# A graph network kernel: the last block's low halves laid beside its high halves

## The reference

```
edge_index = [src, dst]
# layer 0
msg  = (x[src] + rel_emb[type]) @ W_msg.T + b_msg
agg  = segment_sum(msg, dst) / max(deg, 1)
x    = layernorm(x + x @ W_self.T + b_self + agg)
# layers 1 and 2
h    = swish(segment_mean(x[src], dst) @ W1_l.T + b1 + x @ W1_r.T)
y    =       segment_mean(h[src], dst) @ W2_l.T + b2 + h @ W2_r.T
out  = layernorm(x + y)
```

## Time and profile before

| | |
|---|---|
| median of 3 runs | 366.36 us (366.32 to 366.43) |
| the profiled execution | 366.51 us, its span 364.7 us |
| PE busy | 335.0 us (92%), 3385 products |
| DVE busy | 232.8 us (64%) |
| ACT busy | 173.9 us (48%) |
| granted TensorE clock | 1.0 in nearly the whole span |

### The profile page before, as it was taken

How to read it: one execution, slowest core, us unless ns; L and a number is a source line. 1 busy time by engine, 2 the same in 40 slices (tenths; PEclk the granted TensorE clock), 3 DMA queues, 4 the chain that set the end, 5 groups by cost and what they waited for, 6 DMA issues and landing times.

```text
span 364.7 us, 9187 instructions
## 1 busy us (share of the span) xinstructions
PE 335.0 (92%) x3385; PEld 250.4 (69%) x3385; DVE 232.8 (64%) x597; ACT 173.9 (48%) x385; POOL 4.9 (1%) x17
## 2 busy tenths in 40 slices
PE   0689999999999999999999999999999999999970
PEld 0579998998998998998984454555474455455460
DVE  6999988998999999999446942330345031431454
ACT  1585667769778878778522141331252131121040
POOL 5000000000000000000000000000000000000000
PEclk9999999999999999999999999999999999999997
DMA  4700000000000000000000000000000001100102
GB/s 138 171 2 4 2 2 3 4 2 4 2 2 2 3 4 3 3 2 2 24 16 3 0 0 2 0 2 0 0 2 3 0 1 31 29 2 29 30 2 67
DMA packets 8523, 5.38 MB, mean 15 GB/s; under 512 B 370, under 2 KB 8476, under 8 KB 8476
## 3 DMA queue, kind: packets, MB, share of 16 engines
q1 hardware_dynamic: 8188, 4.32, 4.4%
q10 hardware_dynamic: 288, 0.43, 0.3%
HBM read 3.14 MB, written 1.60 MB: 13 GB/s over the span
## 4 chain that ended last, share of the span: by engine, by line
PE 84%; DVE 8%; ACT 4%; issue 2%; DMA 1%; ACTq 0%; DVEq 0%
PE ps L943 54%; PE ps L891 16%; PE ps L1009 5%; PE ps L1019 3%; PE ps L962 2%; ACT counts L834 2%; DVE hot L1182 1%; PE ps L989 1%; DMA counts<-dst_t 1%; PE ps L898 1%; PE ps L908 1%; DVE hot L1175 1%; DVE table L1192 1%; ACT new_first L812 1%; ACT scaled L790 1%
## 5 line engine op out<-in xcount | busy, mean ns | idle before, releaser
L943 PE MATMUL ps<-counts,table 128*128 128x256 f16 (+2 forms) x1350 | 214.6, 309 | 0.0
L943 PEld LDWEIGHTS ps<-counts,table 128*128 128x128 f16 x1350 | 114.9, 97 | 74.2 <-issue 0.2
L834 ACT CAST counts<-ps 128x494 f32 x208 | 107.7, 578 | 45.5 <-PE ps L891 44.9
L891 PE MATMUL ps<-hot 128*128 128x156 f16 (+1 forms) x584 | 67.9, 241 | 15.6 <-DVE hot L1182 15.0
L891 PEld LDWEIGHTS ps<-hot 128*128 128x128 f16 x584 | 53.1, 103 | 17.3 <-DVE hot L1182 15.3
L1182 DVE TENSOR_TENSOR hot<-iota,edges 128x1200 f16<-128x1200 f16 x73 | 56.6, 775 | 0.0
L1175 DVE TENSOR_TENSOR hot<-iota,edge_rows 128x768 f16<-128x768 f16 x73 | 40.1, 550 | 4.9 <-PE ps L928 4.6
L898 PE MATMUL ps<-window_hot,hot 128*128 128x19 f16 x292 | 42.5, 181 | 0.0
L1272 DVE TENSOR_TENSOR new_first<-ps,scaled 128x512 f32<-128x512 f32 (+1 forms) x9 | 5.4, 600 | 54.0 <-ACT scaled L790 54.0
L1272 DVE TENSOR_TENSOR hot<-ps,scaled 128x512 f32<-128x512 f32 (+1 forms) x8 | 5.1, 639 | 41.6 <-ACT scaled L790 41.6
L898 PEld LDWEIGHTS ps<-window_hot,hot 128*128 128x128 f16 x292 | 28.9, 99 | 0.7
(11 more groups left out here) (135 smaller groups left out, 320.3 us busy)
## 6 DMA issues: line engine op xcount, KB each, us to landing
table<-x SPq DMA_DIRECT2D x2, 768.0 KB, 5.1
out<-new_first SPq DMA_DIRECT2D x3, 256.0 KB
out<-hot SPq DMA_DIRECT2D x3, 256.0 KB, 2.4
counts<-first_dst ACTq DMA_DIRECT2D x1, 208.0 KB, 3.9
counts<-dst_t SPq DMA_DIRECT2D x1, 208.0 KB, 4.5
counts<-type_t ACTq DMA_DIRECT2D x1, 208.0 KB, 4.7
counts<-src_t SPq DMA_DIRECT2D x1, 208.0 KB, 5.0
hot<-w_l SPq DMA_DIRECT2D x2, 64.0 KB, 2.0
```

What stands on the lines that cost most here:

```text
L834: nc.scalar.copy(A[:, HALVES[half], bass.ds(bases[group % 8], GROUP_W)], window(group, half)).then_inc(copied[half], 1)
L891: return nc.tensor.matmul(window(group, half)[:, :, at[t]], row(tiles[t], LOW_AT, P), blocks_of(tiles[t], half), start=group == half == t ...
L943: last = nc.tensor.matmul(ps[:, sums_bank(q), first:first + width], table[:, b, part, :], A[:, b, at:at + width], start=b == part == 0, st ...
```

## The change

The last block's low half for the 53 nodes goes to rows 64 to 116 of the table's high part, so that one product over 128 rows covers both halves; for that the counts of rows 0 to 52 of the last block are copied to rows 64 to 116 by a DMA, once layer 0 no longer needs the relation counts that stood there. PE waits for the copy (semaphore `stacked`) ahead of the last block of chunk 7. In the later layers the last block then has one product in `aggregate`, and the turn of a 53-node chunk has one product, with an identity in which both halves stand (`ident_stacked`), made by one DVE instruction.

```
--- before.py
+++ after.py
@@ -246,7 +246,9 @@
         checks = later[:, 4 * D + 2 * CHUNK:4 * D + 2 * CHUNK + TILES]
         steps = later[:, 4 * D + 2 * CHUNK + TILES:4 * D + 2 * CHUNK + TILES + GROUPS]
         bias_last = later[:, 4 * D + 2 * CHUNK + TILES + GROUPS:][:, 0:D]
-        assert 5 * D + 2 * CHUNK + TILES + GROUPS <= (SLOTS - 1) * HOT_C * GROUP // 2
+
+        ident_stacked = later[:, 5 * D + 2 * CHUNK + TILES + GROUPS:].bitcast(F16)[:, 0:LAST]
+        assert 5 * D + 2 * CHUNK + TILES + GROUPS + P // 4 <= (SLOTS - 1) * HOT_C * GROUP // 2
 
         ident = new_first[:, 0:P]
         bias_msg = scaled_flat[:, 0:D]
@@ -281,9 +283,10 @@
             return (table1, table0)[layer_of(q)]
 
         def table_rows(table, q, part):
+
             first = chunk_of(q) * SUB
             if tiles_of(q) == 1:
-                return table[0:LAST, first, part, :]
+                return table[part * REL_ROW:part * REL_ROW + LAST, first, 0, :]
             return table[:, first:first + SUB, part, :]
 
         ps = ctx.enter_context(nc.psum_tensor("ps", [P, 8, 512], F32))
@@ -325,6 +328,7 @@
         x_in = [sem(f"x_in{k}") for k in range(2)]
         weights_in = sem("weights_in")
         late_weights_in = sem("late_weights_in")
+        stacked = sem("stacked")
         constants = sem("constants")
         pads_zero = sem("pads_zero")
         cleared = sem("cleared")
@@ -709,6 +713,13 @@
             sp.dma_start(bias_last, b2.rearrange("o d -> (o d)").partition_broadcast(P)
                          ).then_inc(late_weights_in, 16)
 
+
+
+            sp.wait_ge(agg_done, CHUNKS)
+            sp.wait_ge(deg_done, CHUNKS)
+            sp.dma_start(A[REL_ROW:REL_ROW + LAST, BLOCKS - 1, 0:N], A[0:LAST, BLOCKS - 1, 0:N]
+                         ).then_inc(stacked, 16)
+
             for q in range(2 * CHUNKS, ALL_CHUNKS):
                 sp.wait_ge(rows_ready, q + 1)
                 first = chunk_of(q) * CHUNK
@@ -939,11 +950,15 @@
                         pe.wait_ge(lo_ready, (layer_of(q) - 1) * CHUNKS + b // SUB + 1)
                     if b == first == 0 and summed_before(q) >= 0:
                         pe.wait_ge(sum_ready, summed_before(q) + 1)
-                    for part in range(2):
+                    both = q >= CHUNKS and b + 1 == BLOCKS
+                    if both and q == CHUNKS:
+                        pe.wait_ge(stacked, 16)
+                    for part in range(1 if both else 2):
                         last = nc.tensor.matmul(
                             ps[:, sums_bank(q), first:first + width], table[:, b, part, :],
                             A[:, b, at:at + width], start=b == part == 0,
-                            stop=b + 1 == BLOCKS and part == 1, skip_group_check=True)
+                            stop=b + 1 == BLOCKS and (both or part == 1),
+                            skip_group_check=True)
                     if b + 1 == BLOCKS and first + width == nodes:
                         last.then_inc(agg_done, 1)
 
@@ -956,13 +971,17 @@
                     pe.wait_ge(x_lo, (chunk_of(q) * SUB + SUB - 1) // X_PIECE + 1)
                 elif turn_bank(q) == messages_bank(q - 1):
                     pe.wait_ge(messages_scaled, q)
+                both = q >= CHUNKS and tiles_of(q) == 1
+                if both:
+                    pe.wait_ge(weights_ready, 4)
                 for t in range(tiles_of(q)):
                     size = min(P, nodes_of(q))
-                    for part in range(2):
+                    for part in range(1 if both else 2):
                         last = nc.tensor.matmul(
                             ps[:, turn_bank(q), t * P:t * P + size],
-                            table_in(q)[:, chunk_of(q) * SUB + t, part, :], ident_h[:, 0:size],
-                            start=part == 0, stop=part == 1, skip_group_check=True)
+                            table_in(q)[:, chunk_of(q) * SUB + t, part, :],
+                            ident_stacked if both else ident_h[:, 0:size],
+                            start=part == 0, stop=both or part == 1, skip_group_check=True)
                 last.then_inc(turned, 1)
 
             def count_degrees(q):
@@ -1452,6 +1471,9 @@
                     preset(POSTED)
 
             wait_copied(dve, GROUPS)
+            nc.vector.tensor_tensor(ident_stacked, ident_h[:, 0:LAST],
+                                    ident_h[:, REL_ROW:REL_ROW + LAST], ALU.add
+                                    ).then_inc(weights_ready, 1)
             nc.vector.memset(table1[32:REL_ROW, BLOCKS - 1], 0.0)
             nc.vector.memset(table1[REL_ROW:P, BLOCKS - 1], 0.0)
             for q in range(EARLY - 1, ALL_CHUNKS):
```

## The result

| | median | runs | ratio to before, 95% interval |
|---|---|---|---|
| before | 366.18 us | 16 | |
| changed | 369.50 us | 16 | 1.0094 [1.0073, 1.0115] |

The change makes the kernel 3.3 us slower; 368.5 us was forecast, from 366.4 to 371.5. The profiled executions differ by 3.2 us (369.67 against 366.51; spans 367.9 and 364.7). Line 957 is now the aggregation, 1028 and 1038 the dense products, 980 the turn. So beside the medians stands a second measure, which the groups don't touch: the time in the profiled execution from the first product of chunk 7 to the last restart of PE with eight products (191.33 to 352.68 us before, 161.35 us).

A forecast was written before the change was run, and what follows sets the result against it. PE's own work, mainly the aggregation, was taken to bound the later layers. Products removed -2.59, wait +3.4 and clock +1.35 sum to +2.2 us: 368.5 us against the 366.36 us median, range 366.4 to 371.5 us.

The forecast's parts named there:

- products removed: Chunks 7 to 12 and 14 to 19: one product of 0.216 us fewer each, all on the path, -2.59 us.
- the wait for the copy: PE at chunk 7's last block: wants the copy at 202.37 us, restarts at 205.8 us, +3.4 us.
- the clock: In or just behind PE's wait: falls to half for 2.7 us of products at double pitch, +1.35 us.
- the last steps: End of the kernel, behind PE's last restart: no term in the prediction, counted at 0.
- The two short chunks: Chunks 13 and 20, 53 nodes each: their savings only lengthen PE's idle time, counted at nothing; 0.1 us without that cover.
- VectorE's sum: Ahead of clearing the table at 179.98 us: 128 x 53 values, hidden by 0.81 us idle; at most 0.3 us otherwise.
- The copy on one engine: SP's copy of 53 rows: prime 53 leaves one DMA engine, share 0.06 to 0.07, like the kernel's last store.
- The straight line: Copy's streaming time, fitted through 512- and 1664-byte rows: 247 ns per 6250-byte row, 13.1 us for 53.
- The tail: After the copy's last packet: 0.3 us to landing, then 0.14 us until PE starts again.
- from issue to first packet: Start of SP's copy: 0.8 us, taken from the last 53-row store, first packet at 192.25 us.
- The two rates that I held as the long end: Slower paces for the copy: 22 GB/s gives a wait of 5.4 us, 14.6 GB/s one of 13.0 us.
- Rival (a): At chunk 7's last block: the copy waits but the clock holds, +0.8 us, 367.2 us; chance 0.33.

The follow-up runs named there:

- 64 rows: The changed kernel, with the copy taking 64 rows (the last 11 empty counts) instead of 53: 363.71 us, 0.9940 of the kernel before.
- the busy wait: The changed kernel, with 24 products of 384 columns into unused columns ahead of PE's wait for the copy: 367.71 us, 1.0050 of the kernel before.
- the copy alone: The kernel before, with only the 53-row copy and PE's wait for it added, two products per block everywhere: 372.01 us, 1.0164 of the kernel before.
- 59 rows: The changed kernel, copying 59 rows instead of 53: 370.66 us, 1.0128 of the kernel before.
- 58 rows: The changed kernel, copying 58 rows instead of 53: 363.19 us, 0.9923 of the kernel before.
- 54 rows: The changed kernel, copying 54 rows instead of 53: 364.13 us in one run, too few for a ratio.
- chunk 7's columns first: The changed kernel, its copy cut in two: chunk 7's 512 columns, then the rest with its own wait at chunk 8: 363.71 us, 0.9945 of before.

## Why the prediction was right

**Sign, mechanism and order of size were as forecast.** +2.2 us was predicted, +3.3 measured; each term against its measure:

| term | forecast | measured |
|---|---|---|
| products removed | -2.59 | -2.59 up to the last restart, -0.22 a chunk; -2.3 in the medians of 64 rows |
| the wait for the copy | +3.4 | +4.0 |
| the clock | +1.35 | +1.7 (the busy wait: 1.8 by medians, 1.66 by starts) |
| the last steps | 0 | +0.15 |
| sum | +2.2 | +3.3 |

**The saving.** 10.80 to 10.58 us a chunk is what one product fewer should give. Twelve make 2.59 us, and up to PE's last restart that is what the 64-row kernel gained, to 0.01 us; the medians show 2.3 us, with 1.2 to 3.2 as its interval. The two short chunks give nothing, their idle time is as long or longer: as forecast. Behind the last restart the span (taken to 0.01 us) goes on for 12.06 us before and 12.05 in the copy alone, but for 12.18 to 12.25 in the kernels with the stacked rows. The prediction had nothing for these 0.12 to 0.19 us, 0.15 in the table; what makes them was not tried. VectorE's sum took 0.19 us and its idle time shrank from 0.81 to 0.58: covered, as forecast.

**The copy on one engine.** The argument from the 53-row store held, and the numbers of rows around 53 show that it is the divisor and not the size: 53 rows 0.07, 59 rows 0.07 (over 192.80:207.20), 58 rows 0.14, 54 rows 0.54, 64 rows 0.86.

**The wait's size: the step that was mis-sized is the start.** The straight line gave 13.1 us of streaming; the packets run from 192.7 to 205.9 us, 13.2 us. The tail (0.3 + 0.14 us) was 0.45 us. But "from issue to first packet ... I take 0.8" was 1.3 us (191.40 to 192.7): the issue itself takes 0.69 us on SP, where the 53-row store took 0.26. That is 0.5 of the 0.6 us by which the wait was longer; that the longer issue makes the later start is not shown. The two rates that I held as the long end (22 and 14.6 GB/s) were too low: 331,250 bytes in 13.2 us is 25.1 GB/s (the 27 GB/s of the row 192.70:205.88 hold code packets too), where the straight line has 25.3.

By the Trainium skill's ceiling for the fabric (DMA: Bandwidth & Descriptors, "Where 436 GB/s comes from") the estimate was 27.2 GB/s for an engine and 12.2 us for the stream. The trace has 25.1 GB/s, under the ceiling, and a stream 1.0 us longer.

**The clock.** It fell, as the likelier case said, and cost 1.7 us and not 1.35: it was at half for 3.4 us of full work, not the 2.7 that I estimated. It fell at 206.5 us, that is just behind the wait and not in it, so that all of its time at half was paid for. The way to the estimate did not hold: I took the time at half to be as long as the idleness before the fall, but it was 3.4 us in the changed kernel, in the copy alone and with 59 rows, where PE had idled 3.9, 3.9 and 4.7 us before the fall. That 1.35 came near 1.7 is in part luck. Rival (a) (the clock holds) is what the kernel with the busy wait makes, 367.7 us, where 367.2 was given. The granted clock of the kernel before needs care at its start: it reads 1.00 from 20 to 28 us, while the products of the earlier trace rows took 312 ns in that stretch, the length that they have at 0.50 in the other profiles (315 ns from 22 to 24 us in the kernel with chunk 7's columns first); the product lengths that I read were the better guide.

**What stays open.** Why one DMA engine's copy starts 1.3 us behind its issue. What adds the 0.15 us at the end. Whether the forecast wait of 3.4 us would have made the clock fall. Whether single runs of the changed kernel left the wait without a fall: only one execution has a profile, but none of the 16 runs took less than 367.79 us, 3.3 us over the lowest of the kernel before (364.51), so nothing speaks for it.

## What to carry to other kernels

A partition count is part of the speed of a DMA from SP's queue: before a DMA whose landing is on the path, look at how many engines a transfer with that row count kept busy in the profile, and pad the rows to a number that more engines divide (64 here, and 54 or 58 were enough), or put the first-needed columns first. A saving that adds a wait is to be set against landing minus arrival, and to a wait of TensorE such as this one of 4.0 us the fall of the clock (here 1.7 us) is to be added. The change's worth lay in one row number: 53 gives +3.3 us, 64 gives -2.3. And where single runs fall in groups, a stretch of the profile between two fixed points shows what medians blur.

## What the hardware showed that I had not expected

- The same 53-row copy kept one DMA engine busy from SP's queue (0.07) and most of them from GpSimd's (0.68).
- One more row, 54 for 53, cut the copy from 13.2 us to about 2.3.
- The clock fell after the wait was over, at 206.5 us, 4 us after the last product had ended at 202.5; in the copy alone it fell at 207.6 us, 1.0 us after PE had started again. At the end of the kernel before it had fallen 2.7 us after the last product. Products of 384 columns in the wait kept it.
- The groups 1.7 us apart arise ahead of chunk 7. In the profiled execution of the kernel with chunk 7's columns first (362.38 us, its lower group) the clock is at half for some 3 us while the counts are built, in that with the busy wait (367.97 us, its middle group) for some 10 us:

```profile
21.50:24.70 3.20, 2.86 (x32) 2.72 (x30) 3.20 (x7) 2.55 (x5) 0.00 (x0) 0.50 0.03 5
24.90:29.00 4.10, 3.86 (x55) 3.58 (x56) 4.10 (x10) 2.45 (x6) 0.00 (x0) 1.00 0.01 4
```

```profile
19.20:29.30 10.10, 8.74 (x83) 8.42 (x82) 9.94 (x20) 6.19 (x11) 0.00 (x0) 0.50 0.01 2
```

The first of them begins chunk 7 at 189.64 us and the second at 191.33; the kernel before at 191.33 as well, and every other profiled execution between 191.00 and 191.51. These rows don't hold all of the time at half: ahead of them the column reads 1.00, but in the first kernel the 144-column products take 313 ns until 17.8 us and 238 ns from 18.2 us on.

```profile
L905 PE MATMUL ps<-hot 128*128 128x144 f16 x8 | 1.6, 313 | 0.0
```

```profile
L905 PE MATMUL ps<-hot 128*128 128x144 f16 x4 | 0.5, 238 | 0.0
```

So the place of the difference is shown, and that the clock differs there from execution to execution; that the clock makes the groups is likely and was not tried.
